# A linear-attention recurrence on one core: GpSimd's weighting of k is released by another instruction of VectorE

## The reference

```python
q, k, v = xn @ Wq, xn @ Wk, xn @ Wv
beta = sigmoid(xn @ Wb + bb)
q = layernorm(silu(causal_dwconv(q, qconv_w, qconv_b)), qn_w, qn_b)   # per head
k = layernorm(silu(causal_dwconv(k, kconv_w, kconv_b)), kn_w, kn_b)
S = (1 - b) * S + b * (v_t outer k_t);  o_t = S @ q_t                 # scan over tokens
s = (o * silu(xn @ Wg)) @ Wo
x = x + s * silu(ffn(xn))
```

## Time and profile before

| | us |
|---|---|
| median of 3 runs | 2605.1 (2599.21 to 2606.36) |
| the profiled execution, its own time | 2600.33 |
| span of its trace | 2598.5 |
| TensorE busy (PE) | 2456.1 |
| VectorE busy (DVE) | 1904.5 |
| ScalarE busy (ACT) | 1241.8 |
| GpSimd busy (POOL) | 849.1 |

### The profile page before, as it was taken

How to read it: one execution, slowest core, us unless ns; L and a number is a source line. 1 busy time by engine, 2 the same in 40 slices (tenths; PEclk the granted TensorE clock), 3 DMA queues, 4 the chain that set the end, 5 groups by cost and what they waited for, 6 DMA issues and landing times. The chain is left out here.

```text
span 2598.5 us, 43686 instructions
## 1 busy us (share of the span) xinstructions
PE 2456.1 (95%) x14784; PEld 2175.3 (84%) x14784; DVE 1904.5 (73%) x3396; ACT 1241.8 (48%) x2025; POOL 849.1 (33%) x442
## 2 busy tenths in 40 slices
PE   4889989989999999999999999996999998999997
PEld 4778878889999989999989999996788887888886
DVE  5589999989999999999999999998422123432232
ACT  5455455545555656555555555554533223322221
POOL 1245544433434343443434343444000000221220
PEclk9999999999999999999999999998999999999999
DMA  7566566576655675666676656664551102431320
GB/s 283 166 212 212 194 221 221 201 263 205 215 195 211 210 274 195 211 218 205 210 249 231 200 204 210 211 208 142 180 204 49 65 32 73 151 121 45 113 90 23
DMA packets 242375, 462.74 MB, mean 178 GB/s; under 512 B 59382, under 2 KB 162038, under 8 KB 221178
## 3 DMA queue, kind: packets, MB, share of 16 engines
q10 hardware_dynamic: 107648, 244.34, 27.3%
q1 hardware_dynamic: 125946, 192.21, 22.0%
q0 software_dynamic: 8704, 25.19, 3.1%
HBM read 371.99 MB, written 98.07 MB: 181 GB/s over the span
## 5 line engine op out<-in xcount | busy, mean ns | idle before, releaser
L1023 DVE SCALAR_TENSOR_TENSOR xn_rows<-ps_proj,conv,xn_rows 128x1021 f32<-128x1021 f32 x381 | 486.8, 1278 | 11.6 <-ACT xn_rows L900 2.5
L1221 PE MATMUL ps_proj<-xt_hi,w_hi 128*128 128x512 f32 x1008 | 409.0, 406 | 20.1 <-DMA xt_lo<-scratch_xt_lo 12.0
L1223 PE MATMUL ps_proj<-xt_hi,w_lo 128*128 128x512 f32 x1008 | 398.5, 395 | 0.0
L1222 PE MATMUL ps_proj<-xt_lo,w_hi 128*128 128x512 f32 x1008 | 397.1, 394 | 0.0
L784 POOL TENSOR_TENSOR rc_k_state<-rc_tok_k,k_norm_rows 128x1024 f32<-128x1024 f32 x64 | 153.6, 2400 | 599.6 <-DVE rc_q_silu L1035 511.9
L1243 PE MATMUL ps_proj<-wv_hi,xt_hi 128*128 128x256 f32 x1024 | 295.2, 288 | 0.7 <-PEq L75 0.7
L1244 PE MATMUL ps_proj<-wv_lo,xt_hi 128*128 128x256 f32 x1024 | 289.8, 283 | 0.0
L1245 PE MATMUL ps_proj<-wv_hi,xt_lo 128*128 128x256 f32 x1024 | 289.8, 283 | 0.0
L1221 PEld LDWEIGHTS ps_proj<-xt_hi,w_hi 128*128 128x128 f32 x1008 | 191.9, 190 | 59.1 <-DMA xt_lo<-scratch_xt_lo 13.3
L1653 DVE TENSOR_TENSOR ff_wide_lo<-ff_wide,ff_wide_hi 128x512 fp32r<-128x512 f32 x64 | 44.4, 693 | 248.7 <-ACT ff_wide_hi L1568 248.7
L1223 PEld LDWEIGHTS ps_proj<-xt_hi,w_lo 128*128 128x128 f32 x1008 | 191.4, 190 | 42.0
(11 more groups left out here) (181 smaller groups left out, 5757.0 us busy)
## 6 DMA issues: line engine op xcount, KB each, us to landing
rc_q_rows<-scratch_rows ACTq DMA_DIRECT2D x64, 1024.0 KB, 5.1
rc_k_rows<-scratch_rows ACTq DMA_DIRECT2D x64, 1024.0 KB, 4.6
rc_decay_all<-scratch_decay ACTq DMA_DIRECT2D x64, 512.0 KB, 5.4
rc_cum_all<-scratch_cum ACTq DMA_DIRECT2D x64, 512.0 KB, 3.7
scratch_o<-rc_o_sb ACTq DMA_DIRECT2D x64, 512.0 KB, 3.5
w_hi<-scratch_w_split SPq DMA_DIRECT2D x48, 512.0 KB, 4.7
w_lo<-scratch_w_split SPq DMA_DIRECT2D x48, 512.0 KB, 5.5
wv_hi<-scratch_wv_split SPq DMA_DIRECT2D x24, 512.0 KB, 3.9
```

The lines of the kernel that those rows point to most:

```text
L1023: nc.vector.scalar_tensor_tensor(out=act_cm[j][:, back:], in0=projected[:, 0:L - back], scalar=conv[par][:, j, t:t + 1], in1=act_cm[j][:, ...
L1221: nc.tensor.matmul(out, hi, xt_hi[:, k, cols], start=k == 0, stop=False)
L1222: nc.tensor.matmul(out, hi, xt_lo[:, k, cols], start=False, stop=False)
L1223: last = nc.tensor.matmul(out, lo, xt_hi[:, k, cols], start=False, stop=k == KC - 1)
```

## The change

In GpSimd's part of a step the weighting of k waits for one semaphore instead of another: for the scan of the same head (`dmat_done`) where it waited for the second pass over q of the same head (`q_scaled`, two counts a head). The other two waits stay.

```diff
--- before.py
+++ after.py
@@ -779,7 +779,7 @@
 
                     k_tokens = k_state[C_.par]
                     after_step(pool, "k_normed", C_.i)
-                    after_step(pool, "q_scaled", C_.i, 2)
+                    after_step(pool, "dmat_done", C_.i)
                     after_step(pool, "updates_mm", C_.i - 2)
                     nc.gpsimd.tensor_tensor(k_tokens[:], tok_k[:], k_norm_rows[:, 0:1].to_broadcast([P, NC, P]),
                                             ALU.mult).then_inc(S["k_weighted"], 1)
```

## The result

The changed kernel takes 2731.5 us in the median of 4 runs (2729.8 to 2734.6), the kernel before 2604.0 (2599.2 to 2606.4): ratio 1.0493, 95% interval 1.0475 to 1.0512. It is slower by 127 us. The forecast was 2710 us, with a range of 2675 to 2760.

The account below looks back on a forecast made before the run. VectorE and TensorE were taken to bound the steady steps together. Steady 87, first steps 10, sequence starts 6 and tail 2 made 105 us on 2600.3 profiled: 2705, or 2710 us against the median 2605.1; range 2675 to 2760.

Parts of the forecast that it names:

- an earlier start is worth nothing in the steady steps: GpSimd's weighting is ready some 2.5 us earlier, but ScalarE's wait for TensorE at L913 hides the gain.
- VectorE has almost no room: Steady steps: 4.5 us of slack over 45 steps, 0.10 a step; net loss 1.93 us a step.
- The two starts of sequences: q 4.3 us late: q_cum goes ahead of L1033, L811 ahead of L1035; 2.8 us each, 6 in all.
- q's rows come no later against VectorE: Steady steps: the transposition they start from moves less than a step's 2 us, so no added lateness.
- no DMA issue is moved past another: GpSimd's queue: the wait on the scan ends before the old one, so the order of DMA issues stays.
- rival 3: GpSimd's weighting goes first in every step, ahead of L1033: 4.6 us a step, 2830 us; chance 0.06.
- 87 + 6: 87 us for 45 steady steps at 1.93 us each, plus 6 us for two sequence starts.
- the first steps: First 15 steps: gains in even steps and losses in odd ones nearly cancel; about 10 us, bounds 0 and 25.
- The tail: Last two steps, where L811 no longer meets k's passes: +2 us.
- Rivals 1 and 2: 1: GpSimd enters after both q passes, 2605 us, chance 0.08. 2: large passes run side by side, 2577 us, 0.04.
- the mean of L784 near 3.4 us: Sign in steady steps: GpSimd's weighting of k averages near 3.4 us instead of 2.40.
- Rival 4: TensorE's clock falls after idle gaps: 2726 us, over 2800 with more than one gap a step; chance 0.06.

Follow-up runs that it names:

- the run that only writes: Changed kernel with GpSimd's weighting of k replaced by setting the tile to a constant, still released by the scan: 2576.0 us, ratio 0.9901 to the kernel before.
- the one released 1.2 us later: Kernel with the weighting of k released by the first of VectorE's two passes over q, not by the scan: 2598.9 us, ratio 0.9989 to the kernel before.
- v's weights held: Changed kernel with SyncE's loads of v's weights held until the store of the rows has landed, from the second sequence on: 2695.7 us, ratio 1.0353.
- the same hold: Kernel before with SyncE's loads of v's weights held until the store of the rows has landed: 2599.7 us, ratio 0.9971.

## Why the prediction was right

**Right, and shown by runs.** That an earlier start is worth nothing in the steady steps: GpSimd's chain ends 2.2 us earlier in the run that only writes, for no gain there. That the loss comes from the meeting of two passes that read SBUF: this run does not lose, and the one released 1.2 us later loses nothing. The order L1033, weighting, L1035, q_cum, taken from one place in the tail, and its price: 2.08 us forecast, (155.1 - 57.6) / 47 = 2.07 us measured against the same passes on k. That VectorE has almost no room: where q's rows are on time in all but two of the steady steps (v's weights held), the 16th and the 62nd scan start at 579.01 and 1841.14, 27.44 us a step; before it was 571.59 and 1744.79, 25.50. The difference is 1.93 us a step, as forecast; against the kernel before with the same hold (25.47) it is 1.97. The two starts of sequences, reckoned at 2.8 us each, grew by 2.5 and 2.7 from scan to scan in the changed kernel.

**The step that failed:** "q's rows come no later against VectorE, because the transposition that they start from moves less than a step's 2 us". The transposition did move less (it comes 1.5 us earlier against the next scan), but the rows are stored and loaded in between, and the store takes 2 us longer now. The statement that no DMA issue is moved past another failed with it: the second load of v's weights now stands ahead of the store. So rival 3 (GpSimd first), which had a chance of 0.06 for all steps, came true in 16 of 47, two of them the starts that the prediction had reckoned so. In the sum: the steady part from the 16th to the 62nd scan (578.65 to 1873.57) grew by 1294.92 - 1173.20 = 121.7 us where 87 + 6 was forecast. Over the 47 steps L1033's standing is 84.5 - 56.8 = 27.7 us of it, and L1033's idle time before it 17.0 - 12.4 = 4.6. The other 89.4 are 1.9 us a step. Without the late rows the kernel takes 2695.7 us, with them 2731.5: the forecast of 2710 lies between, and the range held the time because it left room for steps in which q is late.

**The small terms.** Up to the 16th scan the kernel is 7.1 us later (578.65 against 571.59), where 10 was forecast for the first steps; but 2.7 of it lie ahead of the first scan (137.41 against 134.67), where the change does nothing, so the first steps themselves cost 4.3. The tail adds 131.9 - 7.1 - 121.7 = 3.1, forecast 2. Rivals 1 and 2 are out by L1035's 3.30 us. Of the signs, the mean of L784 near 3.4 us was missed: it is 2.95, for the weighting comes when L1033 has 0.9 us to go and stands only for that, or is first.

**The clock and TensorE's waits.** Rival 4 came true in a small way. From 560 to 1880 us the granted clock is 0.99 in the mean, but read in stretches of 2 us it falls to or near 0.50, the 1.2 GHz level, at seven places, where it did so at two before. At each TensorE had just been idle: from 952 to 954 us it did nothing, and the clock was 0.58 and 0.57 in the two stretches that follow. It cost little, since VectorE's idle time grew by 2 us only. The new idle time of TensorE is not where the prediction put it: 34.2 us of it are 21 waits of up to 2.9 us at L1280, for VectorE's statistics (L1044), and only 7.8 are waits for the convolutions.

## What to carry to other kernels

A wait that no data needs can be what keeps two engines apart: before removing one, look in the whole trace, the tail and the first steps too, for a place where the two instructions do meet, and read the price there. When two passes exclude each other, tenths of a microsecond of issue order decide which engine stands, so let the one with room arrive second (here a release 1.2 us later made GpSimd stand for nothing). And follow what the delayed engine releases: a load that starts 1.5 us later can meet a small store that others wait for.

## What was not expected of the hardware

From the issue of a 16 KB store to that of the load that waits for it took 1.5 to 5.7 us in the median, depending on which 512 KB loads were issued near it: 1.5 and 1.9 with v's weights held (kernel before and changed), 3.7 in the kernel before, 5.7 in the changed one. And a GpSimd instruction that only wrote, 0.95 us for 128x1024 values, ran at no cost beside a VectorE pass of the kind that stops for one that reads. An operation of 0.17 us (L1070) took 1.74 in the mean when GpSimd's split met it.
